# A gated-attention block with a 32-expert layer: every fourth chunk's low part is made by GpSimd instead of VectorE, and the stage orders are written anew

## What is computed

```python
ln = layernorm(layernorm(x)); xn = layernorm(ctx)            # with gains and biases
q = ln @ Wq.T
k, v = concat([xn @ Wkv.T, ln @ Wlkv.T])                      # 512 keys per batch
attn = softmax(mask(rmsnorm(q) * 64**-0.5 @ rmsnorm(k).T))
x = x + tanh(g_xattn) * ((attn @ v) @ Wo.T + bo)
t = layernorm(x)
gate = top4_of_32(sigmoid(t @ expert_sel.T))                  # other gates are 0
scores = relu(einsum('nd,edf->nef', t, keys)) * gate          # 32 experts of 64
x = x + tanh(g_ffn) * einsum('nef,efv->nv', scores, values)
```

## Time and profile before

| what | before |
| --- | --- |
| median of 3 runs | 114.74 us (113.86, 114.74, 114.76) |
| the profiled execution | 113.83 us |
| its span, first to last instruction | 112.0 us |
| around the span | 1.8 us |
| PE busy | 105.6 us (94%) |
| DVE busy | 94.4 us (84%) |
| ACT busy | 65.1 us (58%) |
| POOL busy | 16.0 us (14%) |

### The profile page before, as it was taken

One profiled execution on the slowest core, in us unless ns is written; L12 is line 12 of the kernel. 1 busy time (PEld: TensorE's weight loads), 2 busy tenths in 40 slices (PEclk: granted clock), 3 DMA queues, 4 the chain that ended last, 5 costly groups with the idle time before them and its releaser, 6 DMA issues.

```text
span 112.0 us, 2072 instructions
## 1 busy us (share of the span) xinstructions
PE 105.6 (94%) x644; PEld 85.4 (76%) x644; DVE 94.4 (84%) x307; ACT 65.1 (58%) x145; POOL 16.0 (14%) x27
## 2 busy tenths in 40 slices
PE   4999999889999999999989999999999999999990
PEld 4989889547678797768978766678888888888860
DVE  5788899779977689988596989999999799899951
ACT  4689999998989733294613502636263373644410
POOL 6000016004004666000400800000000000000000
PEclk9999999999999999999999999999999999999998
DMA  3789700000000000000003986466009985763002
GB/s 86 209 232 423 336 6 6 6 0 0 0 0 6 0 0 0 3 0 6 12 12 126 287 283 222 173 235 177 16 18 258 287 296 210 235 180 125 0 0 94
DMA packets 7111, 12.78 MB, mean 114 GB/s; under 512 B 893, under 2 KB 2557, under 8 KB 6846
## 3 DMA queue, kind: packets, MB, share of 16 engines
q1 hardware_dynamic: 7102, 12.67, 34.6%
HBM read 12.00 MB, written 0.66 MB: 113 GB/s over the span
## 4 chain that ended last, share of the span: by engine, by line
PE 79%; DVE 8%; ACT 7%; issue 3%; POOL 0%; DVEq 0%; POOLq 0%
PE bank L729 13%; PE bank L731 13%; PE bank L730 13%; PE bank L867 12%; PE bank L738 6%; PE bank L854 5%; PE bank L921 3%; PE bank L825 2%; DVE junk L453 2%; PE bank L852 2%; PE bank L788 2%; PE bank L813 1%; ACT cx L600 1%; PE bank L807 1%; PE bank L892 1%
## 5 line engine op out<-in xcount | busy, mean ns | idle before, releaser
L706 ACT ACTIVATE hid_hi<-keys 128x512 fp32r<-128x512 f32 x28 | 17.5, 630 | 18.5 <-DVE keys L543 15.3
L543 DVE SCALAR_TENSOR_TENSOR keys<-bank,inT 128x512 f32<-128x512 f32 x32 | 21.1, 685 | 1.3 <-issue 0.6
L560 DVE TENSOR_TENSOR hid_lo<-keys,hid_hi 128x512 fp32r<-128x512 f32 x28 | 18.7, 685 | 0.9 <-ACT hid_hi L706 0.6
L867 PE MATMUL bank<-vw,prob 128*128 128x129 f32 x128 | 15.8, 278 | 0.0
L867 PEld LDWEIGHTS bank<-vw,prob 128*128 128x128 f32 x128 | 14.8, 192 | 0.7 <-issue 0.7
L729 PE MATMUL bank<-xm_hi,k_lo 128*128 128x512 f32 x32 | 14.5, 454 | 0.0
L453 DVE CUSTOM_DVE_ANT_0 junk<-bank,mask_b 128x512 bf16<-128x512 f32 x16 | 10.4, 688 | 3.0 <-PE bank L825 3.0
L731 PE MATMUL bank<-xm_hi,k_hi 128*128 128x512 f32 x32 | 12.5, 391 | 0.0
L730 PE MATMUL bank<-xm_lo,k_hi 128*128 128x512 f32 x32 | 12.5, 390 | 0.0
L729 PE MATMUL bank<-hid_hi,v_lo 128*128 128x512 f32 x28 | 11.2, 399 | 0.0
L731 PE MATMUL bank<-hid_hi,v_hi 128*128 128x512 f32 x28 | 10.9, 391 | 0.0
(11 more groups left out here) (131 smaller groups left out, 197.9 us busy)
## 6 DMA issues: line engine op xcount, KB each, us to landing
inT<-gate_rows SPq DMA_DIRECT2D x32, 256.0 KB, 4.3
keys<-keys_in SPq DMA_DIRECT2D x1, 1024.0 KB, 7.1
values<-values_in SPq DMA_DIRECT2D x1, 1024.0 KB, 9.2
out<-x_mid SPq DMA_DIRECT2D x4, 128.0 KB, 2.3
vecs_x<-x_in SPq DMA_DIRECT2D x1, 256.0 KB, 4.4
wa<-wa_in SPq DMA_DIRECT2D x1, 208.0 KB, 2.8
cx<-ctx_in SPq DMA_DIRECT2D x2, 96.0 KB, 2.7
cx<-ctx_in SPq DMA_DIRECT2D x1, 192.0 KB, 5.0
```

Of the source, the lines that this page charges most:

```text
L543: dve.scalar_tensor_tensor(hid[:, n % 3, :], bank[H_BANK[n % len(H_BANK)]][:, :], 0.0, gated[:, n % SLOTS, :], ALU.max, ALU.mult).then_inc ...
L560: dve.tensor_tensor(hid_lo[:, m % RING, :], hid[:, n % 3, :], hid_hi[:, m % RING, :].bitcast(F32), ALU.subtract).then_inc(hid_lo_ready, 1)
L706: act.activation(hid_hi[:, m % RING, :], hid[:, n % 3, :], ACT.Copy).then_inc(hid_hi_ready, 1)
L867: last = pe.matmul(bank_of(b, OUT + t)[:, WOA * a:WOA * a + WOA], prob[:, b % 2, a, j, P * t:P * t + P], vw[:, b, j, a, :], start=(j == 0) ...
```

## The change

Of the 28 split chunks those with m % 4 = 3 (m = n - 4) get their low part from POOL: chunks 0.7, 0.11, 0.15, 1.3, 1.7, 1.11 and 1.15, seven in all. They have a semaphore of their own (`pool_lo_ready`), and whoever waits for a low part asks the semaphore of its maker. The inverse roots are refined on DVE as before. All four orders are written anew: on POOL, ACT, DVE and PE the same stages stand, except for the seven splits, which leave DVE's list and enter POOL's.

```diff
+POOL_SLOT = RING - 1
...
 POOL_ORDER = """
-    low_keys 0, mask 0, low_keys 1, low_keys 2, scale_bo 0, add_bias 0, low_keys 3, add_bias 1, low_values 0,
-    low_values 1, low_values 2, low_values 3
+    low_values 0, mask 0, low_values 1, low_keys 0, low_keys 1, scale_bo 0, add_bias 0, add_bias 1, low_keys 2,
+    low_keys 3, split 0.7, low_values 2, split 0.11, low_values 3, split 0.15, split 1.3, split 1.7, split 1.11,
+    split 1.15
...
+        def wait_low(engine, m):
+
+            if m % RING == POOL_SLOT:
+                engine.wait_ge(pool_lo_ready, m // RING + 1)
+            else:
+                engine.wait_ge(hid_lo_ready, m + 1 - (m + 1) // RING)
...
+            def split(h, c):
+                n = EC * h + c
+                m = n - WHOLE
+                pool.wait_ge(hid_ready, n + 1)
+                pool.wait_ge(hid_hi_ready, m + 1)
+                if m >= RING:
+                    pool.wait_ge(down_done, n - RING + 1)
+                pool.tensor_tensor(hid_lo[:, m % RING, :], hid[:, n % 3, :], hid_hi[:, m % RING, :].bitcast(F32),
+                                   ALU.subtract).then_inc(pool_lo_ready, 1)
...
-                    dve.wait_ge(hid_lo_ready, n - WHOLE + 1)
+                    wait_low(dve, n - WHOLE)
...
-                    pe.wait_ge(hid_lo_ready, m + 1)
+                    wait_low(pe, m)
```

More of the change, by code:

```diff
@@ L62 @@
[L62 to L70, removed]
+    turn_in 0, warm 13, warm 14, warm 15, warm 16, project 0, fold 0, turn_in 1, warm 17, vctx 0, warm 18,
@@ new lines @@
+    project 1, warm 19, vlat 0, warm 20, vctx 1, turn_in 2, warm 21, vlat 1, turn_qk 0, vctx 2, warm 22, warm 23,
+    vlat 2, turn_in 3, row_max 0.0, project 2, row_max 0.1, turn_qk 1, vctx 3, vlat 3, turn_max 0, row_max 1.0,
+    weights 0.0, row_max 1.1, project 3, turn_qk 2, weights 0.1, turn_max 1, row_max 2.0, weights 1.0,
+    attend 0.0, row_max 2.1, attend 0.1, turn_max 2, turn_qk 3, weights 1.1, weights 2.0, row_max 3.0,
+    attend 1.0, row_max 3.1, attend 1.1, turn_mid 0, weights 2.1, turn_max 3, weights 3.0, select 0, attend 2.0,
@@ new lines @@
+    turn_mid 1, weights 3.1, turn_gates 0, select 1, attend 2.1, turn_gates 1, attend 3.0, attend 3.1, up 0.0,
+    turn_mid 2, up 0.1, select 2, turn_res 0, turn_res 1, up 0.2, up 0.3, down 0.0, down 0.1, up 0.4, down 0.2,
+    up 0.5, turn_mid 3, down 0.3, up 0.6, up 0.7, select 3, up 0.8, down 0.4, up 0.9, up 0.10, down 0.5, up 0.11,
+    down 0.6, turn_gates 2, up 0.12, down 0.7, up 0.13, turn_gates 3, down 0.8, down 0.9, up 0.14, up 0.15,
+    down 0.10, turn_res 2, down 0.11, up 1.0, up 1.1, down 0.12, down 0.13, up 1.2, down 0.14, up 1.3, down 0.15,
@@ L82 @@
+    norm_qk 2, row_max 1.1, sum_qk 3, turn_max 1, row_max 2.0, norm_qk 3, row_max 2.1, turn_max 2, out_proj 0,
+    stats_mid 0, row_max 3.0, norm_mid 0, row_max 3.1, out_proj 1, turn_max 3, stats_mid 1, turn_mid 0,
     norm_mid 1, select 0, turn_mid 1, select 1, out_proj 2, stats_mid 2, norm_mid 2, out_proj 3, turn_mid 2,
-    stats_mid 3, up 0.0, up 0.1, up 0.2, select 2, up 0.3, up 0.4, norm_mid 3, split 0.4, up 0.5, up 0.6, up 0.7,
-    split 0.5, split 0.6, up 0.8, split 0.7, turn_mid 3, up 0.9, split 0.8, up 0.10, select 3, split 0.9,
@@ L85 @@
[L85 to L89, removed]
+    stats_mid 3, up 0.0, up 0.1, norm_mid 3, up 0.2, up 0.3, select 2, up 0.4, up 0.5, turn_mid 3, split 0.4,
@@ L90 @@
+    up 0.6, up 0.7, split 0.5, split 0.6, up 0.8, up 0.9, up 0.10, select 3, split 0.8, split 0.9, up 0.11,
+    up 0.12, split 0.10, up 0.13, up 0.14, split 0.12, split 0.13, up 0.15, split 0.14, up 1.0, up 1.1, up 1.2,
+    split 1.0, split 1.1, split 1.2, up 1.3, up 1.4, up 1.5, split 1.4, up 1.6, split 1.5, up 1.7, split 1.6,
+    up 1.8, up 1.9, split 1.8, up 1.10, split 1.9, split 1.10, up 1.11, up 1.12, up 1.13, split 1.12, up 1.14,
+    up 1.15, split 1.13, split 1.14, finish 1
 """
 ACT_ORDER = """
-    stats_in 0, norm_in 0, constants 0, stats_in 1, turn_in 0, norm_in 1, fold 0, project 0, stats_in 2,
@@ L93 @@
[L93 to L102, removed]
@@ L103 @@
-    split 1.14, split 1.15
+    stats_in 0, constants 0, norm_in 0, turn_in 0, stats_in 1, project 0, norm_in 1, fold 0, turn_in 1,
+    stats_in 2, vctx 0, sum_qk 0, project 1, split_keys 0, stats_in 3, norm_in 2, split_values 0, vlat 0, vctx 1,
+    turn_in 2, vlat 1, turn_qk 0, sum_qk 1, norm_in 3, round_qk 0, vlat 2, split_values 1, vctx 2, turn_in 3,
+    project 2, turn_qk 1, round_qk 1, vlat 3, sum_qk 2, vctx 3, weights 0.0, split_values 2, project 3,
+    turn_qk 2, round_qk 2, weights 0.1, sum_qk 3, weights 1.0, split_keys 1, split_keys 2, turn_qk 3, round_qk 3,
@@ new lines @@
+    weights 1.1, stats_mid 0, weights 2.0, turn_mid 0, split_keys 3, weights 2.1, stats_mid 1, weights 3.0,
+    select 0, turn_mid 1, select 1, weights 3.1, turn_gates 0, turn_gates 1, stats_mid 2, turn_mid 2,
+    split_values 3, stats_mid 3, select 2, turn_mid 3, split 0.4, split 0.5, split 0.6, split 0.7, select 3,
+    split 0.8, split 0.9, turn_gates 2, turn_gates 3, split 0.10, split 0.11, split 0.12, split 0.13, split 0.14,
+    split 0.15, split 1.0, split 1.1, split 1.2, split 1.3, split 1.4, split 1.5, split 1.6, split 1.7,
@@ L104 @@
+    split 1.8, split 1.9, split 1.10, split 1.11, split 1.12, finish 0, split 1.13, split 1.14, split 1.15
 """
@@ L364, in add_bias @@
                                    ALU.add).then_inc(bias_ready, 1)
-            run = {"mask": mask, "scale_bo": scale_bo, "add_bias": add_bias,
+            run = {"mask": mask, "scale_bo": scale_bo, "add_bias": add_bias, "split": lambda at: split(*at),
                    "low_keys": lambda q: low_part(q, keys, k_hi, k_lo, keys_hi_ready, keys_lo_ready),
```

14 lines of the change are left out of this document (5 added, 9 removed).

## The result

The changed kernel takes 116.06 us (median of 116.02, 116.03, 116.10 and 116.76); the runs of the kernel before beside it have a median of 114.52 us. The ratio is 1.0165, 95% interval 1.0121 to 1.0208: slower, by some 1.9 us (the two medians alone differ by 1.54). Forecast were 114.3 us and no change, the range ended at 115.8, so both missed. The profiled execution took 116.02 us with a span of 114.2 us, 2.2 us more than that of the profiled execution before, which was among the fastest of its kernel.

A forecast was written before the change was run, and what follows sets the result against it. PE was taken to bound the expert half; -0.8 for the attention orders, 0 for the moved splits and +0.4 for the tail gave -0.4, so 114.3 us from the median 114.74. Range 113.7 to 115.5; for 8 in 10, 112.8 to 115.8.

The forecast's parts named there:

- What bounds the kernel: Expert half: PE is the bound at 0.227 us per matmul, DVE has 0.16 us of slack per chunk.
- Parts 1 and 2: Expert half: seven splits moving from DVE to POOL free 4.2 us of DVE but gain 0; DVE waits 0.2 us.
- The two engines together: DVE instructions with both operands in SBUF and POOL's block each other; 0 taken in expert half, bounds 0 to +4.4.
- The forecast's sign: Expert half: single DVE splits stretched to over 0.9 us, each ending with a POOL split.
- Part 3, the tail: Last chunk's low part on POOL stalls PE at its very end: +0.4 us, bounds 0.2 to 0.7.
- POOL in the attention half: POOL's work is the same and `add_bias 0` is ready at 38.3, just before DVE asks at 38.5: 0 taken.
- Part 4, the orders of the attention half: New attention-half orders change only PE's waits: -0.8 us, bounds -2.4 to +1.2.
- +0.45 at `attend 0.0`: Attention half: counting stages still to be done, the new order is 0.45 us behind at `attend 0.0`.
- -1.0 for waits behind it: Attention half after `attend 0.0`: waits with restarts fall from about 2.4 us to 1.4, -1.0.
- -0.25 at `turn_mid 2`: End of attention half: `up 0.0` covers PE's wait for the norm at `turn_mid 2`, -0.25 us.
- Rival (d): Seven splits don't move the end, attention order loses +0.8: sum +1.2, 115.9 us; chance 7%.
- Rival (b): Expert half: the lock between DVE and POOL slows the kernel, sum +1.0, 115.7 us; chance 7%.

The follow-up runs named there:

- e4: Kernel before with the seven low parts made by nobody, `down` multiplying the high part in their place: 114.55 us, ratio 1.0008.
- e2: Kernel before's attention orders with the changed kernel's expert orders and its seven low parts on POOL: 114.34 us against 114.22, ratio 1.0006.
- e8: Changed kernel with the low part of chunk 1.15 back on DVE: 115.72 us, ratio 1.0126 to the kernel before.
- e5: Changed kernel with POOL's long attention-half operations put where DVE has nothing to be held: 115.32 us, ratio 1.0098 to the kernel before.
- e11: Kernel before, orders untouched, with POOL's `add_bias 0` delayed so that it falls on `shift_c`: 114.61 us against 114.54, ratio 0.9999.
- e12: e5 with the kernel before's lists up to `attend 0.0` (PE), `norm_qk 3` (DVE), `round_qk 3` (ACT): 114.76 us against 114.54, ratio 1.0044.
- e6: e5 with `vctx 1` and `split_values 0` on ACT moved behind `round_qk 0`: 115.71 us, ratio 1.0115 to the kernel before.
- e7: Kernel before with ACT's `constants 0` ahead of `norm_in 0` and `turn_in 0` ahead of `stats_in 1`: 114.17 us against 114.3, ratio 0.9996.

## Why the prediction was wrong, point by point

**What bounds the kernel: right.** PE stays full at 0.227 us a matmul, and e4 wins nothing with seven low parts gone.

**Parts 1 and 2: right.** 0 each. DVE waited 0.47 and 0.43 us for POOL's low parts at 84.62 and 89.73, where 0.2 was worked out; PE saw none of it, as e2 shows.

**The two engines together, in the expert half: right.** Holds came in both directions, as forecast, and PE saw none of them. DVE's timeline, then POOL's:

```profile
94.29 1.18 DVE L577 TENSOR_TENSOR hid_lo<-keys,hid_hi 128x512 fp32r<-128x512 f32 x1
```

```profile
75.11 1.55 POOL L365 TENSOR_TENSOR hid_lo<-keys,hid_hi 128x512 fp32r<-128x512 f32 x1 [24.65 <-ACT hid_hi L723]
...
93.62 1.30 POOL L365 TENSOR_TENSOR hid_lo<-keys,hid_hi 128x512 fp32r<-128x512 f32 x1 [4.02 <-ACT hid_hi L723]
```

The split issued at 94.29 was held until POOL's ended at 94.92 (93.62 + 1.30) and then did its own 0.55 us of work, up to 95.47. The forecast's sign had such splits end with POOL's; here only instructions of a few columns did. POOL's at 75.11, with 1.55 us, ran beside a pair of DVE splits (74.22 to 75.50).

**Part 3, the tail: right.** +0.4 was taken; the gap is 0.29 and e8 gives 0.34 back.

**"POOL in the attention half": wrong, 0 taken, 0.86 us measured (e5).** I asked only whether `add_bias` would be ready in time for `out_proj 0`, and not what it would hold while it ran. In my walk `add_bias 0` ran from about 37.0 to 38.3, in truth the pair ran from 38.52 to 41.02; in either case it lay near `shift_c` on DVE, and the question was never put. The cause is one sentence of the part on the two engines together: "a DVE instruction with both operands in SBUF waits for POOL, one with a PSUM operand does not". The two rows behind it leave open what one with a single SBUF operand does, and I read the rule as if `shift_c` were safe. 1.17 us at 38.65 and 0.75 in e11 show that it isn't, and the 0.49 us of the statistics at 41.98 that not every such instruction is held. That `add_bias 0` would be ready in time for `out_proj 0` did come true; it was the wrong question.

The Trainium skill, in "SBUF — State Buffer", section "Who interferes with whom", had the other half of the rule: VectorE takes the shared pair also in its two-port modes, which copies, casts and `tensor_scalar` can enter if their operands fit, while an instruction with at most one SBUF input outside those modes does not contend. By that, the trace agrees in both cases: `shift_c` is a `tensor_scalar` with source and result in SBUF, the statistics are none. Which mode `shift_c` ran in no row shows.

**Part 4, the orders of the attention half: wrong, -0.8 taken, +0.98 measured besides the hold.** Of its three terms two failed and one came out by luck.
- *+0.45 at `attend 0.0`*: it came out as forecast, 34.79 + 0.66 for `turn_qk 3` = 35.45 against 35.01, but by two errors that cancel. `attend 0.0` came at 34.79 and not at 33.7, and `weights 1.1` stands behind it in both kernels, so its 1.1 us should not have been added. The part from there on started from a walk that was already 1.1 us too fast.
- *-1.0 for waits behind it*: I put the kernel before's at 2.4 us, of which one row, 0.38 at 56.65, was shown. The waits view lists 0.6 us in two waits from 35 us on; what restarts cost beside them I had no row for, so a gain of 1.0 rested on none. Even with the hold gone nothing was won: e5's waits from 20 to 65 us sum up to 1.6 us, as before. The wait for `gate` stayed at 0.4, and the one for `shift_r` behind `turn_max 3` grew from 0.2 to 0.4.
- *-0.25 at `turn_mid 2`*: the gap went, and `select 2` waited 0.38 us for DVE at 64.44; e2 puts the whole passage at +0.02.

Of the +0.98, 0.65 us go when the start is the kernel before's (e12). In the changed kernel the scores begin at 21.82 instead of 21.22, since ACT has `split_values 0`, `vctx 1` and `norm_in 3` ahead of `round_qk 0`: the forecast had this step nearly right (21.4; `round_qk 0` ended at 21.77), yet let the time be made good later. (In the kernel before, `round_qk 0` was done at 20.09 and PE was late itself, by 0.49 us for the `cx` of `norm_in 3` in the waits view.) The two changes of ACT's start that were tried, e6 and e7, moved no time to the end. Which of the moved stages carries the 0.65 us stays open. Of the 0.33 of the rest, 0.24 is there by `attend 1.1` (44.38 against 44.14); which stage costs it stays open too.

The rows sum up to 0.86 + 0.65 + 0.33 + 0.29 = 2.13 us, of 2.2 in the span; the first three make 1.84 by the way they were measured, so only the tail is checked by the sum. Rival (d) was the one that came nearest, 115.9 us, "a plain misfit of the new lists"; it had 7%, and its sign, a first unrounded `down` after 65, is what came. But its number is half luck: it has no hold in it, and the hold is 0.86 of the 1.84 us. Rival (b) had a hold, but in the expert half, where none reached PE. The bounds of part 4 reached +1.2; its own +0.98 lies inside, the 1.84 with the hold does not.

## What to carry to other kernels

A gain that rests on a list walked over 40 us is worth no more than its error, and the waits that it removes must each be a row: where the waits view lists 0.6 us, do not count on a reordering to win 1.0. Where GpSimd has wide operations, write beside each the VectorE instructions that fall into it and are of the kinds that get held, and ask of each what TensorE has between it and its user: a hold of `shift_c` cost 0.86 us with one stage in between, and one of 0.57 us cost nothing with three. Work taken off an engine with slack was worth nothing here, even removed altogether (e4); leave the last piece before the end on the engine that is quicker at it.
